# Edge passes of a four-layer graph network: scores and tile maxima of a batch moved into the step before, and a plain running maximum in layer 0

## The chip, the core and the metric

The program runs on one core of one Trainium2 chip. The metric is the device time of one execution in microseconds (us). The engines are PE (matmul; its weight loads are shown as PEld), DVE, ACT, POOL and SP; each runs its own list of instructions in order, and they meet only at semaphores.

## The reference, cut to what matters

A model of four layers works on 3125 nodes of 256 features, with 50000 edges. Each layer adds an edge part, a dense attention part and an expert or MLP part. The change touches only the edge parts that have a softmax over the edges of each node: layer 0 (a directional message, score from the message), layer 1 (dot product of query and key), and the two attention layers of layer 3. In layer 0:

```
messages = (x @ Wf.T)[src] * direction[:, :1] + (x @ Wr.T)[src] * direction[:, 1:2]
scores = leaky_relu(einsum('ef,hf->eh', messages, attn_forward[0]), 0.2)
exp_scores = exp(scores - scores.max(axis=0, keepdims=True))     # one maximum per head, over all edges
sum_exp = segment_sum(exp_scores, dst)
out = segment_sum(messages * exp_scores / (sum_exp[dst] + 1e-10), dst)
```

Layers 1 and 3 instead subtract the maximum over the edges of each node (`segment_max`), exponentiate, and divide by the node's sum.

## The kernel before, in words

The edges have been sorted by node into 416 tiles of 128 edge slots; a tile belongs to one bucket of 128 nodes, and a bucket may begin several tiles. One function, `edge_pass`, runs all four passes: `kind` is "dual" in layer 0 (4 heads), "dot" in layer 1 (8 heads, 32 wide), "add" in L3a (4 heads) and L3b (1 head, 256 wide). A batch is SB = 8 tiles, so there are NB = 52 batches, and a step of the unrolled loop (`steps`) handles one new batch `n` and, LAG = 2 steps later (1 in "dot"), its sums. In each step:

- POOL gathers the rows of 8 tiles by indirect transfer (L1288) into a ring of RING = LAG + 2 slots. A slot is free once the sums of the batch in it are done (`summed`), in "dual" once its message is made (`used`).
- DVE makes the scores (`score_rows`, L1311 to L1339); in "dot" that is a product and a reduction over 2048 columns, in "add" three small instructions, after key matmuls on PE; in "dual" three products and sums over 544 columns.
- PE turns the scores (`turn_scores`, L1488); DVE takes a forward and a backward maximum scan within each tile (`tile_maxima`, L1346, L1347); PE brings the tile maxima to one row (`row_maxima`, L1494 to L1496); DVE scans that row, which carries the open node's maximum from batch to batch (`chain_maxima`, L1354 to L1365); PE brings it back as columns (`column_maxima`, L1503); DVE widens it over the tile (`widen`, L1371 to L1373); PE turns it back (`turn_back`, L1509), DVE subtracts (`lower`, L1380, L1381), ACT exponentiates and weighs (L1622, L1632; on DVE L1391).
- ACT also makes the factor by which old sums fall when the maximum rises (L1614, L1616); PE spreads it (`spread_factor`, L1519, L1520), DVE applies it (`rescale`, L1399).
- For the old batch PE forms 8 tile sums (`sums`, L1533), each into one of BANKS banks, and DVE adds each to the accumulator (`merge`, L1409); a bank is free when its merge is done.
- SP loads the masks of tile borders ("walls", L1273, L1275).

All steps of a batch's maximum, from scores to lowering, lie in one step. The order on DVE is: scores, rescale, merge 0, tile maxima, (weigh), chain, merges 1 and 2, widen, merges 3 and 4, lower, the rest. The order on PE is: as many sums as there are banks, turn, row maxima, one sum, keys, column maxima, two sums, turn back, factor, the rest. In L3b (`guest`) the layer's message MLP runs beside the pass: PE does its whole share of a step between the first three sums and the turn, and BANKS is 3. In "dot" PE also expands query rows (L1482), which ACT copies out (L1607). The order on each engine is written out by hand.

Of the kernel before, what the change touches and what calls it, by code (L numbers as in the profile page):

```python
# [26 lines left out]
ds = bass.ds  # L27
# [15 lines left out]
SB = 8  # L43
# [1101 lines left out]
def edge_pass(kit, name, kind, order, row_table, key_rows, heads, width, acc, guest=None):  # L1145
# [26 lines left out]
    ROW = P  # L1172
    COL = ROW + H * SEQ
    BACK = COL + 2
    KEYS = RING * H
    with Stage(kit, name) as s:
# [4 lines left out]
        hot = s.sb("hot", [P, RING, SB, P])  # L1181
        wall = s.sb("wall", [R, 2, P + 1])
        chain_wall = s.sb("chain_wall", [1, 2, H * SEQ + 1])
        score_all = s.sb("score_all", [P, P])
        score = score_all[:, 0:R]
        shifted = s.sb("shifted", [P, R])
        runs = s.sb("runs", [R, P])
        tops = s.sb("tops", [P, P])
# [4 lines left out]
        ends = s.sb("ends", [1, 2, P])  # L1193
        column = s.sb("column", [R, 2])
        fall = s.sb("fall", [1, H])
        factor = s.sb("factor", [1, H])
        minus = s.sb("minus", [1, 1])
        if kind == "dual":
            dirs = s.sb("dirs", [P, 2, ST])
            msg = s.sb("msg", [P, 2, SB, HALF])  # L1200
            msg2 = s.sb("msg2", [P, SB, HALF])
            rhs = s.sb("rhs", [P, RING, SB, M])
# [25 lines left out]
        def share(units, c):  # L1228

            if beside and 0 <= c < NB:  # L1230
                for _ in range(beside.UNITS * (c + 1) // NB - beside.UNITS * c // NB):
                    next(units)

# [17 lines left out]
        with nc.Block() as block:  # L1251

            @block.sync
            def _(sp):
# [8 lines left out]
                for n in range(NB):  # L1263
                    b = n % 2
                    if keyed:
                        if n >= 2:
                            sp.wait_ge(columns_hot, n - 1)
                        sp.dma_start(lo_rows[:, b, :], order["lo_rows"][n * SB:(n + 1) * SB, :]
                                     .rearrange("t p -> (t p)").partition_broadcast(P)).then_inc(lined[b], 16)
                    if n >= 2:  # L1270
                        sp.wait_ge(widened, n - 1)
# [21 lines left out]
            def _(dve):  # L1293
# [11 lines left out]
                def score_rows(n, c, ring_turn):  # L1305
                    g = rows[:, c % RING]
                    out = by_head(score)
                    dve.wait_ge(gathered[c % RING], ring_turn * (16 * SB) + 16 * SB)
                    if kind == "dot":
# [3 lines left out]
                        if c >= 1:  # L1313
                            dve.wait_ge(lowered, n)
                        v.tensor_reduce(out, g[:, :, 0:KW].rearrange("p k (h v) -> p k h v", h=H), X,
                                        ALU.add).then_inc(scored, 1)
                    if kind == "add":
                        dve.wait_ge(expanded, n * 2 + 2)
                        if c >= 1:
                            dve.wait_ge(factored, n)  # L1320
                        if c >= 1:
                            dve.wait_ge(lowered, n)
# [3 lines left out]
                        v.scalar_tensor_tensor(out=score, in0=score, scalar=0.2, in1=score, op0=ALU.mult,  # L1326
                                               op1=ALU.max).then_inc(scored, 1)
                    if kind == "dual":
                        if c >= 2:
                            dve.wait_ge(weighed_act, n - 1)  # L1330
                        link.note(v.tensor_tensor(msg[:, c % 2], g[:, :, 0:HALF],
                                                  bcast(dirs[:, 0, ds(n * SB, SB)], HALF, 2), ALU.mult))
                        link(v.tensor_tensor(msg2[:], g[:, :, HALF:RW], bcast(dirs[:, 1, ds(n * SB, SB)], HALF, 2), ALU.mult))
                        m = msg[:, c % 2]
                        v.tensor_tensor(m, m, msg2[:], ALU.add).then_inc(used, 1)  # L1335
                        dve.wait_ge(used, n + 1)
                        if c >= 1:
                            dve.wait_ge(lowered, n)
# [3 lines left out]
                def tile_maxima(n, c, wall_turn):  # L1342
                    b = c % 2
                    dve.wait_ge(walled[b], wall_turn * (16 * (H + 1)) + 16 * (H + 1))
                    dve.wait_ge(turned, n + 1)
                    link(v.tensor_tensor_scan(runs[:], wall[:, b, 0:P], ps_a[0:R, 0:P], -BIG, ALU.add, ALU.max))  # L1346
# [2423 lines left out]
```

## Time and profile before

| | us |
|---|---|
| timed runs, median of 3 (lowest, highest) | 8171.8 (8169.69, 8186.81) |
| span of the profiled execution, first to last instruction | 8112.0 |
| profiled execution's own time | not given apart from the span |
| PE, DVE, ACT, POOL busy (share of the span) | 5601.5 (69%), 4057.9 (50%), 2838.0 (35%), 3138.4 (39%) |
| mean granted TensorE clock, share of 2.4 GHz | 0.800 |

Busy time is the time in which an engine executes; the rest it waits or is being given work. The profile is of one execution. Its shares are means over stages with different limits, so the edge passes have to be read from windows of their own. Lines such as L1409 are lines of the kernel; a pass is told from another by the names (L_edges is layer 0 between 1130 and 1900 us and layer 1 between 2838 and 3646 us; L3a_edges and L3b_edges are the others).

### The profile page before, as it was taken

Reading aid. Unit: us, or ns where it says so; the run is one execution under the profiler, and the core shown is the slowest. Engines: PE = TensorE matmul, PEld = TensorE weight load, DVE = VectorE, ACT = ScalarE, POOL = GpSimd, SP = SyncE. Lnnn points to the kernel's source line nnn. Section 1 sums busy time; section 2 is a strip of 40 time slices with the busy share of each in tenths; the row PEclk is TensorE's granted clock in tenths of the full one; section 3 lists DMA queues with packets and bytes.
Section 4 is the critical chain, followed back from the end, with each engine's and each line's share of the span. In section 5 each row is a group of like instructions: output and inputs, shape, how many; then the busy total and the mean of one; then the engine's idle time right before and its main releaser. Section 6 shows DMA issues by size and latency. Waiting matters only on the chain. (4 is left out here: it accounts for less than half of the span.)

```text
span 8112.0 us, 86982 instructions
## 1 busy us (share of the span) xinstructions
PE 5601.5 (69%) x21290; PEld 3555.5 (44%) x21290; DVE 4057.9 (50%) x9795; ACT 2838.0 (35%) x7825; POOL 3138.4 (39%) x3209
## 2 busy tenths in 40 slices
PE   2222547677699778887785568698857866888576
PEld 1111325445355356653343345354545543555343
DVE  5325836665311389994434333423456675555501
ACT  4223627664122144430102333122246633555110
POOL 3663035553466166640005662100056634555011
PEclk9999965557799878778997778799956666787588
DMA  2221521111010255540002221100033423333122
GB/s 84 69 65 42 173 66 43 40 39 16 26 32 20 74 157 159 160 129 14 8 27 87 84 85 39 38 33 30 14 103 106 110 66 92 89 91 90 54 109 69
DMA packets 272398, 573.85 MB, mean 71 GB/s; under 512 B 87398, under 2 KB 138138, under 8 KB 265242
## 3 DMA queue, kind: packets, MB, share of 16 engines
q0 software_dynamic: 134496, 314.63, 15.5%
q1 hardware_dynamic: 137530, 254.96, 9.6%
q8 instruction: 148, 2.42, 0.1%
q14 instruction: 224, 1.84, 0.1%
HBM read 520.14 MB, written 49.19 MB: 70 GB/s over the span
## 5 line engine op out<-in xcount | busy, mean ns | idle before, releaser
L1288 POOL DMA_INDIRECT L_edges_rows<-scratch_L_kv,L_edges_index x416 | 491.1, 1180 | 392.5 <-PE L_edges_ps_sum L1533 221.5
L1288 POOL DMA_INDIRECT L3a_edges_rows<-scratch_L3a,L3a_edges_index x416 | 442.6, 1064 | 472.7 <-DMA L3a_edges_last<-order_dst_last 256.7
L1288 POOL DMA_INDIRECT L3b_edges_rows<-scratch_L3b,L3b_edges_index x416 | 396.8, 954 | 460.1 <-PE L3b_edges_ps_sum L1533 296.7
L1288 POOL DMA_INDIRECT L_edges_rows<-scratch_L,L_edges_index x416 | 416.4, 1001 | 372.2 <-DVE L_edges_msg L1335 199.2
L1730 POOL TENSOR_TENSOR L_norm_fold<-L_norm_square 128x400 f32<-128x400 f32 x64 | 66.5, 1040 | 1262.2 <-ACT L_norm_square L1739 1262.2
L676 POOL DMA_INDIRECT L_edges_rows<-scratch_L,L_edges_index x416 | 396.8, 954 | 394.2 <-SPq L660 145.6
L499 POOL DMA_INDIRECT scratch_by_dst<-dst_record,dst_dest x400 | 406.2, 1016 | 315.0 <-DVE dst_dest L338 195.6
L518 POOL DMA_INDIRECT scratch_by_src<-src_record,src_dest x400 | 387.7, 969 | 266.9 <-issue 110.1
L688 PE MATMUL L_edges_ps_sum<-L_edges_rows,L_edges_hot 128*128 128x256 f32 x832 | 271.1, 466 | 222.7 <-issue 122.8
L400 PE MATMUL rank_ps_count<-rank_parts,rank_ident_b 128*128 128x225 bf16 x200 | 53.6, 370 | 534.6 <-DVE rank_parts L312 423.9
L2376 DVE TENSOR_TENSOR L_experts_gated_h<-L_experts_hidden,L_experts_share_rows 128x800 f32<-128x800 f32 x112 | 111.0, 992 | 609.5 <-ACT L_experts_hidden L2366 535.0
L1409 DVE TENSOR_TENSOR L_acc<-L_edges_ps_sum,L_acc 128x264 f32 (+1 forms) x832 | 357.1, 429 | 97.1 <-DVE L_acc L1409 57.5
L2366 ACT ACTIVATE L_experts_hidden<-L_experts_ps_h,L_eb_sb 128x400 f32<-128x400 f32 x320 | 187.6, 593 | 613.8 <-PE L_experts_ps_h L2328 499.7
L1533 PE MATMUL L_edges_ps_sum<-L_edges_rhs,L_edges_hot 128*128 128x264 f32 x832 | 395.4, 640 | 0.3 <-DVE L_acc L1409 0.3
L1533 PE MATMUL L3a_edges_ps_sum<-L3a_edges_rows,L3a_edges_hot 128*128 128x264 f32 x832 | 373.6, 610 | 1.4 <-DVE L_acc L1409 1.3
L728 DVE TENSOR_TENSOR L_acc<-L_edges_ps_sum,L_acc 128x256 f32 x416 | 176.7, 425 | 380.8 <-DMA scratch_L<-L_table_row 177.4
L464 ACT ACTIVATE rank_apart<-x,rank_key_f 128x128 bf16<-128x128 f32 x800 | 244.4, 388 | 301.2 <-remote 239.1
L2339 PE MATMUL L_experts_ps_o<-L_experts_gated_h,L_e_sb 128*128 128x400 f32 x896 | 330.9, 511 | 23.9 <-DVE L_experts_gated_h L2376 23.9
L1533 PE MATMUL L3b_edges_ps_sum<-L3b_edges_rows,L3b_edges_hot 128*128 128x258 f32 x832 | 333.9, 553 | 5.1 <-DVE L_acc L1409 4.9
L2328 PE MATMUL L_experts_ps_h<-xn,L_e_sb 128*128 128x400 f32 x896 | 323.0, 504 | 2.1 <-PEq L113 2.1
L1596 ACT ACTIVATE L_edges_hot<-iota,L_edges_lo 128x128 f32<-128x128 f32 x832 | 254.7, 386 | 161.9 <-DMA L_edges_last<-order_src_last 92.1
L688 PEld LDWEIGHTS L_edges_ps_sum<-L_edges_rows,L_edges_hot 128*128 128x128 f32 x832 | 173.7, 226 | 313.2 <-issue 178.9
(761 smaller groups left out, 13494.6 us busy)
## 6 DMA issues: line engine op xcount, KB each, us to landing
x<-scratch_dst_key_rows SPq DMA_DIRECT2D x50, 512.0 KB
x<-scratch_src_key_rows SPq DMA_DIRECT2D x50, 512.0 KB
L_experts_w<-in_L_w SPq DMA_DIRECT2D x16, 1024.0 KB
L_edges_rows<-scratch_L,L_edges_index POOLq DMA_INDIRECT x832
L_edges_lo_rows<-order_src_lo_rows SPq DMA_DIRECT2D x52, 256.0 KB
L3a_edges_lo_rows<-order_dst_lo_rows SPq DMA_DIRECT2D x52, 256.0 KB
L3b_edges_lo_rows<-order_dst_lo_rows SPq DMA_DIRECT2D x52, 256.0 KB
x<-scratch_dst_lo_rows SPq DMA_DIRECT2D x50, 256.0 KB
```

Of the source, the lines that this page charges most:

```text
L464: ins = nc.scalar.activation(apart[:, u, k, :], key_line[:, u, k * P:(k + 1) * P], ACT.Abs, scale=-1.0, bias=key_f[:, ds(n * SB + k, 1)])
L499: pool.indirect_dma_start(order["table"], bass.IndirectOffsetOnAxis(order["dest"][:, t:t + 1], 0), order["record"][:, t, :], None).then_in ...
L518: pool.indirect_dma_start(self.order["table"], bass.IndirectOffsetOnAxis(self.order["dest"][:, t:t + 1], 0), self.order["record"][:, t, :] ...
L676: pool.indirect_dma_start(rows[:, n % RING, k, :], None, row_table, bass.IndirectOffsetOnAxis(index[:, t:t + 1].bitcast(U32), 0)).then_inc ...
L688: nc.tensor.matmul(ps_sum[:, k % 4, 0:F], hot[:, n % RING, k, :], rows[:, n % RING, k, :], start=True, stop=True).then_inc(summed, 1)
L1288: pool.indirect_dma_start(rows[:, n % RING, k, 0:RW], None, row_table, bass.IndirectOffsetOnAxis(index[:, t:t + 1].bitcast(U32), 0)).then_ ...
L1409: v.tensor_tensor(a, ps_sum[:, (c * SB + k) % BANKS, 0:M], a, ALU.add).then_inc(merged, 1)
L1533: nc.tensor.matmul(ps_sum[:, (c * SB + k) % BANKS, 0:M], hot[:, c % RING, k, :], values(c)[:, k, :], start=True, stop=True).then_inc(summe ...
L1596: ins = nc.scalar.activation(hot[:, c % RING, k, :], kit.iota[:], ACT.Abs, scale=-1.0, bias=lo[:, ds(n * SB + k, 1)])
L2328: ins = nc.tensor.matmul(ps_h[:, (a + o) % 4, 0:CW], weights[l][:, e, f, o * P:(o + 1) * P], r, start=f == 0, stop=f == len(src) - 1)
L2339: nc.tensor.matmul(ps_o[:, o, 0:CW], weights[hid][:, e, f, o * P:(o + 1) * P], gated_h[:, n % 2, f, :], start=e == 0 and f == 0, stop=False)
L2366: nc.scalar.activation(hidden[l][:, n % 2, o, :], ps_h[:, a % 4, 0:CW], func, bias=biases[l][:, n % EX, o:o + 1]).then_inc(taken, 1)
```

## The change

For every kind, the scores and the tile maxima of batch n+1 are now made in the step that holds the carried chain of batch n (row scan, columns, widening, lowering) and the sums of batch n-LAG. The turned scores move from bank `ps_a` to `ps_c`, where the spread factor and the key products lie, so PE waits for `maxed` before it writes the factor or the next keys. `score` and `tops` get two buffers, `msg` three. `RING` grows by one in L3a only. Key columns, query expansions and their copies run one batch further ahead. `row_maxima` waits for `listed` (the end of `lower`) of the batch before. In L3b the MLP's share of a step is cut into two halves on PE.

In "dual" (layer 0) the maximum is no longer one per node: a running maximum per head over all batches so far replaces it. One reduction takes the place of the two tile scans, one matmul each that of the row and column matmuls, two small instructions that of the chain scans, and the widening, the turn back and the wall loads go.

Core of the diff (long; what is left out renames buffers or changes the prologues in the same sense):

```diff
-    RING = LAG + 2
+    HRING = LAG + 2
+    RING = LAG + 3 if kind == "add" and not guest else HRING
-    AHEAD = 2 if kind == "dot" else 1
+    AHEAD = 3 if kind == "dot" else 2
...
                 def tile_maxima(n, c, wall_turn):
+                    if kind == "dual":
+                        dve.wait_ge(turned, n + 1)
+                        v.tensor_reduce(tops[0:R, b, 0:1], ps_c[0:R, TURN:TURN + P], X, ALU.max).then_inc(maxed, 1)
+                        return
...
                 def chain_maxima(n, c):
                     dve.wait_ge(rowed, n + 1)
+                    if kind == "dual":
+                        old, new = highest[:, 1 - b, :], highest[:, b, :]
+                        link(v.tensor_reduce(new, ps_a[0:1, ROW:ROW + R].rearrange("o (h k) -> o h k", h=H), X, ALU.max))
+                        link(v.tensor_tensor(new, new, old, ALU.max))
+                        if c >= 1:
+                            dve.wait_ge(fell, n)
+                        v.tensor_tensor(fall[:], old, new, ALU.subtract).then_inc(chained, 3)
+                        return
...
# DVE, step
-                    if new:
-                        score_rows(n, c, ring_turn)
                     if old:
                         r = nc.values_load_multi_w_load_instructions(...)
-                        rescale(m, d, r)
-                        merge(m, d, r, (0,))
-                    if new:
-                        tile_maxima(n, c, wall_turn)
-                    if keyed and c + AHEAD < NB:
-                        hot_columns(n + AHEAD, c + AHEAD, wall_turn + (AHEAD + c % 2) // 2)
-                    if LAG == 2 and 1 <= c <= NB:
-                        weigh(n - 1, c - 1)
                     if new:
                         chain_maxima(n, c)
                     if old:
-                        merge(m, d, r, (1, 2))
+                        rescale(m, d, r)
+                        merge(m, d, r, (0,))
+                    if more:
+                        score_rows(n + 1, c + 1, (c + 1) // RING)
+                    if old:
+                        merge(m, d, r, (1,))
                     if new:
                         widen(n, c)
+                    if LAG == 2 and 1 <= c <= NB:
+                        weigh(n - 1, c - 1)
                     if old:
-                        merge(m, d, r, (3, 4))
+                        merge(m, d, r, (2,))
+                    if more:
+                        tile_maxima(n + 1, c + 1, (c + 1) // 2)
+                    if keyed and c + AHEAD < NB:
+                        hot_columns(n + AHEAD, c + AHEAD, (c + AHEAD) // 2)
+                    if old:
+                        merge(m, d, r, (3,))
                     if new:
                         lower(n, c)
                     if LAG == 1 and new:
                         if old:
-                            merge(m, d, r, (5,))
+                            merge(m, d, r, (4, 5))
                         weigh(n, c)
                     if old:
-                        merge(m, d, r, (6, 7) if LAG == 1 and new else (5, 6, 7))
+                        merge(m, d, r, (6, 7) if LAG == 1 and new else (4, 5, 6, 7))
...
# PE: waits
                 def row_maxima(n, c):
                     pe.wait_ge(maxed, n + 1)
+                    if c:
+                        pe.wait_ge(listed, n)
                 def spread_factor(n, c):
+                    if c + 1 < NB:
+                        pe.wait_ge(maxed, n + 2)
# PE, step, after the change
+                    add(0, 1)
+                    column_maxima(n, c)
+                    add(2)
+                    share_part(units, c, True)
+                    expand_pair(n + 2, c + 2, r, 2)      # "dot"
+                    expand_pair(n + 2, c + 2, r, 3)
+                    turn_scores(n + 1, c + 1)
+                    add(3)
+                    turn_back(n, c)                      # not in "dual"
+                    add(4)
+                    spread_factor(n, c)
+                    expand_keys(n + 2, c + 2, r, 0)      # "add"
+                    expand_keys(n + 2, c + 2, r, 1)
+                    row_maxima(n + 1, c + 1)
+                    add(5)
+                    share_part(units, c, False)
+                    add(6, 7)
+                    expand_pair(n + 3, c + 3, r, j)      # "dot", j = 0, 1
...
# ACT, step
-                    if kind == "dot" and c + 1 < NB:
-                        for j in range(4):
-                            copy_asked(n + 1, c + 1, j)
                     if c < NB:
                         fall_factor(n, c)
+                    if kind == "dot" and c + 2 < NB:
+                        for j in range(4):
+                            copy_asked(n + 2, c + 2, j)
+                    if c < NB:
                         weights(n, c)
                         weigh(n, c)
```

## Rows read from the trace of the kernel before

**Rows 1.** Windows of the passes: length, busy PE, PEld, DVE, ACT, POOL, clock, DMA.

```profile
1130.00:1900.00 770.00, 528.69 (x1657) 368.59 (x1657) 488.31 (x1344) 520.78 (x1863) 403.78 (x403) 0.58 0.19 38
...
2838.00:3646.00 808.00, 666.21 (x2463) 482.50 (x2463) 732.65 (x1296) 335.18 (x818) 475.80 (x402) 0.78 0.56 152
...
5930.00:6600.00 670.00, 528.17 (x2053) 377.96 (x2053) 456.22 (x1349) 421.61 (x1446) 420.22 (x393) 0.64 0.40 102
...
6770.00:7550.00 780.00, 669.86 (x2597) 438.60 (x2597) 428.25 (x1367) 420.29 (x1087) 367.97 (x386) 0.78 0.33 83
```

**Rows 2.** Tile sums L1533, one row a pass: ns min/median/max, first and last start.

```profile
L1533 PE MATMUL L_edges_ps_sum<-L_edges_rhs,L_edges_hot x832: 386/647/810, 1174.1 to 1896.9; 128*128 128x264 f32 x167
...
L1533 PE MATMUL L_edges_ps_sum<-L_edges_rows,L_edges_hot x832: 392/393/823, 2858.0 to 3643.9; 128*128 128x272 f32 x167
...
L1533 PE MATMUL L3a_edges_ps_sum<-L3a_edges_rows,L3a_edges_hot x832: 385/647/810, 5954.1 to 6593.0; 128*128 128x264 f32 x167
...
L1533 PE MATMUL L3b_edges_ps_sum<-L3b_edges_rows,L3b_edges_hot x832: 377/636/801, 6792.6 to 7545.7; 128*128 128x258 f32 x167
```

**Rows 3.** Waits of DVE in layer 0: us in total, times, longest.

```profile
DVE L_edges_chain_run L1354 <- DMA x<-scratch_src_key_rows: 51.2, 13, 14.6
```

**Rows 4.** Timeline of layer 0, one pause: start us, length us, idle before.

```profile
1556.00 1.15 ACT L1600 ACTIVATE L_edges_hot<-L_edges_hot,ones 128x1024 f32<-128x1024 f32 x1 [2.19 <-remote]
...
1556.08 0.41 DVE L1346 TENSOR_TENSOR_SCAN L_edges_runs<-L_edges_wall,L_edges_ps_a 32x128 f32<-32x128 f32 x1 [5.96 <-DMA x<-scratch_dst_key_rows]
```

**Rows 5.** Timeline of DVE, a step of layer 0 without pause.

```profile
1505.78 0.71 DVE L1331 TENSOR_TENSOR L_edges_msg<-L_edges_rows,L_edges_dirs 128x544 f32<-128x544 f32 x1
...
1508.76 0.42 DVE L1399 TENSOR_TENSOR L_acc<-L_acc,L_edges_ps_c 128x260 f32 x1 [0.62 <-issue]
...
1510.99 0.28 DVE L1354 TENSOR_TENSOR_SCAN L_edges_chain_run<-L_edges_chain_wall,L_edges_ps_a 1x68 f32<-1x68 f32 x1
...
1511.93 0.41 DVE L1409 TENSOR_TENSOR L_acc<-L_edges_ps_sum,L_acc 128x264 f32 x1
...
1513.10 0.15 DVE L1371 COPY L_edges_column<-L_edges_ps_a 32x2 f32<-32x2 f32 x1
...
1514.20 0.40 DVE L1409 TENSOR_TENSOR L_acc<-L_edges_ps_sum,L_acc 128x264 f32 x1
...
1520.19 0.42 DVE L1399 TENSOR_TENSOR L_acc<-L_acc,L_edges_ps_c 128x260 f32 x1 [0.62 <-issue]
```

**Rows 6.** Timeline of PE in layer 0; two matmul records make one fp32 matmul.

```profile
1503.32 4.77 PE L1533 MATMUL L_edges_ps_sum<-L_edges_rhs,L_edges_hot 128*128 128x264 f32 x10
...
1515.27 0.59 PE L1519 MATMUL L_edges_ps_c<-ones 1*128 1x4 f32 x2
```

**Rows 7.** Timeline of layer 1's start: eighth gather, first use of the batch.

```profile
2827.72 0.95 POOL L1288 DMA_INDIRECT L_edges_rows<-scratch_L_kv,L_edges_index  x1 [0.30 <-issue]
...
2831.55 2.29 DVE L1311 TENSOR_TENSOR L_edges_rows<-L_edges_rows,L_edges_asked 128x2048 f32<-128x2048 f32 x1 [7.46 <-DMA L_edges_rows<-scratch_L_kv,L_edges_index]
```

**Rows 8.** Timeline of layer 1 around lowering.

```profile
3220.43 0.21 DVE L1380 TENSOR_TENSOR L_edges_shifted<-L_edges_score_all,L_edges_ps_a 128x64 f32<-128x64 f32 x1
...
3220.94 1.27 PE L1533 MATMUL L_edges_ps_sum<-L_edges_rows,L_edges_hot 128*128 128x272 f32 x2
...
3221.08 2.28 DVE L1391 TENSOR_TENSOR L_edges_rows<-L_edges_rows 128x2048 f32<-128x2048 f32 x1
...
3222.49 1.70 POOL L1288 DMA_INDIRECT L_edges_rows<-scratch_L_kv,L_edges_index  x1 [1.25 <-PE L_edges_ps_sum L1533]
```

**Rows 9.** Groups of L3a, 6050 to 6500 us: busy us, mean ns, idle.

```profile
L1391 DVE TENSOR_TENSOR L3a_edges_rows<-L3a_edges_rows 128x1024 f32<-128x1024 f32 x35 | 42.2, 1206 | 0.0
...
L1473 PE MATMUL L3a_edges_ps_c<-L3a_sparts,L3a_edges_hot_t 128*128 x280 | 24.5, 175 | 0.5
```

**Rows 10.** Waits of L3b, DVE and PE: us in total, times, longest.

```profile
DVE L3b_edges_runs L1346 <- PE L3b_edges_ps_a L1488: 138.5, 35, 6.3
...
PE L3b_edges_ps_a L1494 <- DVE L3b_edges_tops L1347: 60.2, 44, 4.2
```

More of the change, by code:

```diff
@@ L1232, in share, with share_part, score @@
                     next(units)
+        def share_part(units, c, first):
+            if beside and 0 <= c < NB:
+                count = beside.UNITS * (c + 1) // NB - beside.UNITS * c // NB
+                for _ in range(count // 2 if first else count - count // 2):
+                    next(units)
+        def score(c):
+            return score_all[:, c % 2, :]
         def values(c):
@@ L1306, in score_rows @@
                     g = rows[:, c % RING]
-                    out = by_head(score)
+                    out = by_head(score(c))
                     dve.wait_ge(gathered[c % RING], ring_turn * (16 * SB) + 16 * SB)
@@ L1389, in weigh @@
                     scale = bcast(parts(c)[:, :, act_heads:H, V], V, 3)
-                    src = bcast(msg[:, c % 2, :, 0:V], H - act_heads, 2) if kind == "dual" else out
+                    src = bcast(msg[:, c % 3, :, 0:V], H - act_heads, 2) if kind == "dual" else out
                     v.tensor_tensor(out, src, scale, ALU.mult).then_inc(weighed_dve, 1)
@@ L1454, in _ @@
                 if keyed:
-                    for c in range(AHEAD):
+                    for c in range(2):
                         hot_columns(c, c, 0)
+                score_rows(0, 0, 0)
+                tile_maxima(0, 0, 0)
+                for c in range(2, AHEAD):
+                    if keyed:
+                        hot_columns(c, c, c // 2)
                 steps(step)
@@ L1507, in turn_back @@
                 def turn_back(n, c):
+                    if kind == "dual":
+                        return
                     pe.wait_ge(widened, n + 1)
@@ L1581, in _ @@
                 if kind == "dot":
-                    r = key_registers(1, 0, 4)
+                    r = key_registers(1)
+                    for j in range(4):
+                        expand_pair(1, 1, r, j)
+                turn_scores(0, 0)
+                if kind == "add":
+                    r = key_registers(1)
+                    for j in range(2):
+                        expand_keys(1, 1, r, j)
+                row_maxima(0, 0)
+                if kind == "dot":
+                    r = key_registers(2, 0, 4)
                     for j in (0, 1):
-                        expand_pair(1, 1, r, j)
+                        expand_pair(2, 2, r, j)
                 steps(step)
@@ L1630, in weigh @@
                             out = parts(c)[:, k, h, 0:V]
-                            src = msg[:, c % 2, k, 0:V] if kind == "dual" else out
+                            src = msg[:, c % 3, k, 0:V] if kind == "dual" else out
                             ins = nc.scalar.activation(out, src, ACT.Copy, scale=parts(c)[:, k, h, V:V + 1])
@@ L1635, in step @@
                 def step(n, c, ring_turn, wall_turn):
-                    if kind == "dot" and c + 1 < NB:
-                        for j in range(4):
-                            copy_asked(n + 1, c + 1, j)
                     if c < NB:
                         fall_factor(n, c)
+                    if kind == "dot" and c + 2 < NB:
+                        for j in range(4):
+                            copy_asked(n + 2, c + 2, j)
+                    if c < NB:
                         weights(n, c)
@@ L1649, in _ @@
                 if kind == "dot":
-                    for j in range(4):
-                        copy_asked(0, 0, j)
+                    for c in range(2):
+                        for j in range(4):
+                            copy_asked(c, c, j)
                 steps(step)
```

126 lines of the change are left out of this document (64 added, 62 removed).

## The prediction

> **What bounds the kernel now.** I read the windows of the four edge passes first [rows 1]: they are 3028 us of a span of 8112.0 us, and nothing outside them is touched. None has an engine that is simply full, apart from layer 1, where DVE is busy 732.65 of 808 us. Layer 0's busiest engine is PE with 528.69 of 770, at a mean granted clock of 0.58. So three passes are bound by the order of hand-overs between DVE and PE, and the fourth by DVE's work.
>
> Each pass has 52 batches, one a step, and its tile sums give the step: (1896.9 - 1174.1) / 52 = 13.9 us in layer 0, 15.1 in layer 1, 12.3 in L3a, 14.5 in L3b [rows 2].
>
> In layer 0 most of DVE's idle time stands before the chain scan L1354, 51.2 us in 13 pauses [rows 3], and before the tile scan L1346. The named releaser, a transfer of an earlier stage, is none: L1354 waits for PE alone, which had long finished. Pauses of this sort hit two engines together: DVE comes back at 1556.08 and ACT at 1556.00, the latter before an instruction that waits only for ACT itself [rows 4]. Without a pause DVE's rescale returns after 11.4 us (1508.76 to 1520.19 [rows 5]), so some 2.5 us of the 13.9 are pauses. What causes them I can't read.
>
> The Trainium skill (Runtime: NRT & Kernel Launch, "Instruction fetch mechanics") says that straight code is fetched ahead and a block's crossing is mostly hidden. If so, these pauses aren't fetches and could go wholly; the trace shows no dependence either, and I don't decide by it.
>
> **Layer 0 (dual).** DVE in a step loses: the chain scans with their two copies, 1510.99 to 1511.93 = 0.94 us, for three tiny instructions, which I put at 0.65 (one has at most the length of a scan, at least that of a copy: 0.45 to 0.95); one of two tile scans, 0.41 (the one at 1556.08 [rows 4]); and the widening, 1513.10 to 1514.20 = 1.10 [rows 5]. That is 1.8 us. PE loses a transpose and some of the one-row matmuls, SP its wall loads.
>
> It doesn't follow that the step shortens by 1.8: the new order has a chain of its own. I count from the end of sum 7 of a step, at PE's low clock (1.2 GHz), where a sum takes 4.77 / 5 = 0.95 [rows 6]. DVE merges (to 0.65), the load of the buckets' registers, the 0.62 us idle before 1508.76 [rows 5], now stands here, half of it under the merge (to 0.95), the chain ends at 1.6, rescale and merge 0 at 2.55, the scores of the next batch (1505.78 to 0.62 before 1508.76, so 2.36 [rows 5]) at 4.9. PE has done three sums and the chain's matmul by 3.4 and waits for the transpose until 4.9. Sums 3 and 4 end at 7.25; the factor's four small matmuls (two of them 0.59 [rows 6], all about 0.95) end at 8.2; the row maxima wait for `listed` (7.2) and end at 8.5; sums 5, 6, 7 end at 11.3. At full clock (2.4 GHz) sums cost half, and the step falls to 10.1, where ACT (520.78 / 52 = 10.0 [rows 1]) and POOL (eight times 0.95 + 0.30 [rows 7]) stand. At a clock near 0.65, a little over the 0.58 of before as PE is fuller, I take 11.0 without pauses. So the gain in a smooth step is 0.4 us, not 1.8.
>
> Of the 2.5 us of pauses I keep 1.2: DVE now idles about 2 us in the part where it follows sums 5 to 7 and can be late there, and has fewer instructions. Bounds: all stay (2.5) or none (0). Step 12.2, gain 1.7 x 52 = **-90 us** (-20 to -155).
>
> **Layer 1 (dot).** DVE's work stays as it is, and DVE has next to no waits to lose. But two things get later. (1) Before, sum 5 ran ahead of lowering. Now it stands on PE behind `row_maxima(n+1)`, which waits for `listed(n)`. DVE does merge 4 and then must wait in merge 5, with the weighing of 2.28 us [rows 8] queued behind it, then merges 6, 7 and the next chain. Lowering starts at 3220.43; row maxima could end 0.9 later, a sum takes 0.7 to 1.27 [rows 8], so merge 5 starts at +1.7 to +2.3 instead of +0.95: 1.0 us a step. (2) The ring stays 3 deep while the scores come a step earlier, and sums 5 to 7, which release the last three gathers, come later. With sum 5 at about +1.8, three gathers 1.25 apart end at +5.4, and data lands 2.9 us after an issue ends at the most (2828.67 to 2831.55, the eighth of the first batch [rows 7]): +8.3. DVE wants them at +7.9 (merges and weighing to +5.4, load, chain 1.35, rescale, merge 0). I take 0.3 us (0 to 1.6: a gather of 1.70, as the one at 3222.49 [rows 8], on top). Step 15.1 to 16.4: 1.25 x 52 = **+65 us** (+20 to +150).
>
> **L3a (add).** Chain, tile scans and widening stay, so DVE saves nothing; the ring grows to 5, so gathers keep their lead. The chain as above, with the widening (1.10), a weighing of 1.21 [rows 9] and both tile scans ahead of the factor on PE: `tile_maxima(n+1)` ends at 7.6, factor 8.6, the eight key matmuls at about 0.1 apiece (at most 0.18 [rows 9]) 9.4, row maxima 9.75, sum 7 12.6 at the low clock; at full clock 10.7. At 0.64 [rows 1] this is 12.0 to 12.1, against 12.3: gain 0.4 x 52 = **-20 us** (+30 to -80).
>
> **L3b (add, with the message MLP beside it).** DVE sits idle 138.5 us before the tile scan, since the transpose stands behind the whole share of the MLP on PE, and PE then idles 60.2 us until the scans are through [rows 10]. Halving the share puts PE's work under those scans. PE is busy 669.86 / 52 = 12.9 a step; I count 0.65 of waiting for the chain and 0.35 for the tile maxima of the next batch: 13.9. The ring stays at 4: the last gather, released by sum 7 at 0, issued by 1.85, lands by 4.0 to 4.7, the scores end by 5.4, and PE is busy with the half share until 5.5. That just fits. From 14.5 or 14.6: gain 0.7 x 52 = **-38 us** (+30 to -80).
>
> Prologues do the first scores outside the loop, the same work; three `msg` and two `score` buffers cost nothing. The added wait for `maxed` before the factor is in the chains above.
>
> **Sum.** -90 + 65 - 20 - 38 = -83 us. The profiled span is 8112.0; the median of the timed runs, 8171.8, lies 59.8 above it, and I leave that. 8112.0 + 59.8 - 83 = **8089 us**.
>
> **Rivals.**
> - *The pauses of layer 0 stay whole.* For it: they recur about every second step with the same pattern; against it: L1 has none, with as many DVE instructions. Layer 0 gains 20 instead of 90: 8159.
> - *The waits go wholly, and the clock rises.* PE would be busy 87% of a step of 11.3 in layer 0; layer 1 and L3b, at 82 and 86%, have 0.78 [rows 1]. Then layer 0 takes 10.6 (-172), L3a 11.2 (-57), L3b 13.3 (-62), layer 1 +1.0 (+52): 8172 - 239 = 7933. The Trainium skill (TensorE: Matmul & The Clock Gate, "What's actually happening") has the clock follow PE's recent activity; the trace agrees in that the two fuller passes have the higher clock.
> - *Slower: the late gathers decide.* Where the ring isn't deepened (layer 1, L3b), gathers released by sums 5 to 7 feed scores taken a step earlier. If data lands at lowering + 9.9 (a 1.70 us issue and 2.9 of landing), the wait is 1.9, not 0.3, with merge 5 on top: layer 1 +2.9 x 52 = +150; L3b +30 instead of -38. With layer 0 at -40 and L3a at 0: 8312; with layer 0 at -90: about 8240. It turns the sign from about 0.5 us of waiting in layer 1 if layer 0's pauses stay, and from 1.9 if they go as forecast. For it: POOL in layer 1 takes 475.80 us for 402 gathers, 1.18 each [rows 1]. Against it: on DVE these waits start only after nearly 8 us.
> - That the change doesn't take effect can't be: the order is written out.
>
> **Chances.** Forecast 0.46 (8030 to 8145), pauses stay 0.20, all goes 0.14, late gathers 0.20. Times within 0.2% (16 us), about what can be told from no change, are "same". Faster: 0.45 of the first, 0.10 of the second, 0.14 of the third = 0.69; same 0.01 + 0.08 = 0.09; slower 0.20 + 0.02 = 0.22. The range reaches down to the case in which all goes, and up into the milder part of the slower one: 7930 to 8220.
>
> **What would show it.** Layer 0's sums spaced 12.2 us a batch, with pauses before the chain or the scores; in layer 1 idle time on DVE before merge L1409 with PE as its releaser, some 50 us, and a step over 16; L3b's DVE idle before the tile scan mostly gone, its step under 14.2; L3a within 0.6 of before. I am wrong in the main if layer 1 keeps 15.1 (then 8024), or if layer 0 is below 11 or above 13.4.

## The result: slower by 4.3%, and the profile after

The changed kernel takes 8544.6 us (median of 4 runs, 8526.0 to 8556.2) beside 8178.2 for the kernel before on the same chip: ratio 1.0435 [1.0413, 1.0457]. 8089 was forecast, so the sign was wrong too. The profiled span is 8524.2 us against 8112.0: 412 us more.

The tile sums of the changed kernel (ns min/median/max, first and last start), to be held against [rows 2]:

```profile
L1588 PE MATMUL L_edges_ps_sum<-L_edges_rhs,L_edges_hot x832: 386/644/810, 1167.6 to 1905.2; 128*128 128x264 f32 x167
...
L1588 PE MATMUL L_edges_ps_sum<-L_edges_rows,L_edges_hot x832: 392/497/823, 2879.1 to 4084.5; 128*128 128x272 f32 x167
...
L1588 PE MATMUL L3a_edges_ps_sum<-L3a_edges_rows,L3a_edges_hot x832: 386/644/809, 6404.4 to 7017.2; 128*128 128x264 f32 x167
...
L1588 PE MATMUL L3b_edges_ps_sum<-L3b_edges_rows,L3b_edges_hot x832: 378/383/801, 7220.7 to 7957.1; 128*128 128x258 f32 x167
```

Last start less first start, against [rows 2]: layer 0 +15, layer 1 +420, L3a -26, L3b -17, together +392; the other 21 lie around the passes (13 of them between layer 0's last sum and layer 1's first). By step (a fifty-second): 14.2, 23.2, 11.8, 14.2 us. So the question is layer 1, whose window now reads (columns as in [rows 1]):

```profile
2860.00:4100.00 1240.00, 694.60 (x2452) 497.79 (x2451) 746.96 (x1298) 332.34 (x813) 505.76 (x402) 0.72 0.36 99
```

DVE's busy time barely moved (732.65 in [rows 1]); its waits came. Waits of DVE in that window (us in total, times, longest):

```profile
DVE L_edges_hot_t L1317 <- DMA L_edges_lo_rows<-order_src_lo_rows: 244.9, 49, 6.0
DVE L_acc L1440 <- PE L_edges_ps_sum L1588: 93.7, 57, 2.3
DVE L_edges_rows L1326 <- DMA L_edges_rows<-scratch_L_kv,L_edges_index: 69.5, 50, 3.3
DVE L_edges_runs L1359 <- PE L_edges_ps_c L1529: 40.3, 49, 1.2
```

These four sum to 448 us. The largest stands at an instruction that my prediction never mentions: `hot_columns`, L1317. Timeline of one step, SP's queue and DVE together (start us, length us, idle before):

```profile
3415.37 0.48 DVE L1396 TENSOR_TENSOR_SCAN L_edges_tops<-L_edges_wall,L_edges_column,L_edges_runs 64x128 f32<-64x128 f32 x1
...
3415.88 2.63 SPq L1288 DMA_DIRECT2D L_edges_wall<-order_src_walls  x8
...
3418.55 0.25 SPq L1290 DMA_DIRECT2D L_edges_chain_wall<-order_src_chains  x1
3418.85 0.35 SPq L1281 DMA_DIRECT2D L_edges_lo_rows<-order_src_lo_rows  x1
3422.61 0.75 DVE L1317 TENSOR_SCALAR L_edges_hot_t<-L_edges_lo_rows,node 128x1024 f32<-128x1024 bf16 x1 [4.63 <-DMA L_edges_lo_rows<-order_src_lo_rows]
...
3423.63 0.21 DVE L1409 TENSOR_TENSOR L_edges_shifted<-L_edges_score_all,L_edges_ps_a 128x64 f32<-128x64 f32 x1
...
3426.18 0.44 DVE L1440 TENSOR_TENSOR L_acc<-L_edges_ps_sum,L_acc 128x272 f32 x1 [1.82 <-PE L_edges_ps_sum L1588]
```

SP's loop loads, for each batch, `lo_rows` and then, once the widening of two batches earlier is done, the walls. So `lo_rows` of batch n+3 stands behind `widened` of batch n: it is issued 3.0 us after the widening ends (eight wall issues, one chain issue) and lands by 3.8 us after that. Before, the load went out at the same place of a step, but its user stood in the next step:

```profile
3207.46 0.34 SPq L1268 DMA_DIRECT2D L_edges_lo_rows<-order_src_lo_rows  x1
```

```profile
3215.43 0.72 DVE L1302 TENSOR_SCALAR L_edges_hot_t<-L_edges_lo_rows,node 128x1024 f32<-128x1024 bf16 x1
```

That is 8.0 us of lead (the two rows are from the trace of the kernel before). `AHEAD` 3 in place of 2 moved the user up by a step, and nothing moved the load. In L3a and L3b `AHEAD` is 2 now, the load one step ahead, and no such wait appears.

### The profile page after: what moved, and what is told of

Its sections match the earlier page's. It is cut to its first block and busy times, and to the rows that moved or that the text cites. A ratio compares the mean times of both kernels' runs of the same rounds, so it can differ in the third digit from the quotient of the medians.

```text
span 8524.2 us, 85875 instructions
## 1 busy us (share of the span) xinstructions
PE 5456.9 (64%) x20926; PEld 3363.0 (39%) x20926; DVE 3937.3 (46%) x9479; ACT 2844.9 (33%) x7825; POOL 3170.4 (37%) x3209
## 5 line engine op out<-in xcount | busy, mean ns | idle before, releaser
L1303 POOL DMA_INDIRECT L_edges_rows<-scratch_L_kv,L_edges_index x416 | 523.7, 1259 | 786.7 <-PE L_edges_ps_sum L1588 610.6
L1523 PE MATMUL L_edges_ps_key<-L_q,L_edges_hot_t 128*128 x832 | 314.9, 545 | 228.9 <-ACT L_edges_asked L1673 214.9
L1588 PE MATMUL L_edges_ps_sum<-L_edges_rhs,L_edges_hot 128*128 128x264 f32 x832 | 367.3, 601 | 0.7 <-DVE L_acc L1440 0.7
L1523 PEld LDWEIGHTS L_edges_ps_key<-L_q,L_edges_hot_t 128*128 128x128 f32 x832 | 230.8, 285 | 303.2 <-issue 250.9
L1588 PE MATMUL L3a_edges_ps_sum<-L3a_edges_rows,L3a_edges_hot 128*128 128x264 f32 x832 | 347.8, 563 | 2.3 <-DVE L_acc L1440 1.8
L1698 ACT ACTIVATE L_edges_rhs<-L_edges_msg,L_edges_rhs 128x64 f32<-128x64 f32 x1248 | 320.9, 335 | 83.2 <-issue 67.9
L1588 PE MATMUL L_edges_ps_sum<-L_edges_rows,L_edges_hot 128*128 128x272 f32 x832 | 331.7, 529 | 5.7 <-DVE L_edges_rows L1420 3.4
```

The costliest lines, as they stand in the source:

```text
L1303: pool.indirect_dma_start(rows[:, n % RING, k, 0:RW], None, row_table, bass.IndirectOffsetOnAxis(index[:, t:t + 1].bitcast(U32), 0)).then_ ...
L1523: ins = nc.tensor.matmul(ps_key[:, j % 2, (k % 2) * D:(k % 2 + 1) * D], hot_t[:, c % 2, k * P:(k + 1) * P], key_rows[:, ds(r[k], 1), :].sq ...
L1588: nc.tensor.matmul(ps_sum[:, (c * SB + k) % BANKS, 0:M], hot[:, c % HRING, k, :], values(c)[:, k, :], start=True, stop=True).then_inc(summ ...
L1698: ins = nc.scalar.activation(out, src, ACT.Copy, scale=parts(c)[:, k, h, V:V + 1])
```

## Experiments

Chips differ: the kernel before took 8178, 8097 and 8174 us in three groups of runs and 7290, 7295 and 7292 in three others, each group on one chip. Ratios are always against it on the same chip. The first sort has the pauses of layer 0 that the prediction speaks of, the second has none, and steps of layer 0 are compared only within a sort. Layer 1's step differs little between chips: 15.1 before on both sorts, 23.2 and 23.1 after.

**1. The load alone.** In "dot", SP issues `lo_rows` one batch sooner, ahead of the wait for `widened`.

```
-                    if keyed:  # lo_rows of batch n
+                    ahead = 1 if kind == "dot" else 0
+                    for m in range(n + ahead if n else 0, min(n + ahead + 1, NB)):
...                       # the same wait and load, with m in place of n
```

> The changed kernel with one thing altered: in layer 1 SP issues the 256 KB load of lo_rows for batch n+1 ahead of its wait for the widening of batch n-2, so that it lands a step before hot_columns wants it. Own theory: the 245 us that DVE spends before hot_columns in layer 1 (49 waits of about 5.0 us) are the load's place in SP's queue, 3.0 us behind the end of the widening; they go, and nothing takes their place, so layer 1's step falls from 23.2 to about 18.4 us and the whole from 8545 to about 8300 us. Rival 1, the late gathers decide (they are released by sums 5 to 7 after the lowering): the wait for the load only covered a wait for gathers, the step stays above 22 and DVE's wait at the product L1326 grows from 1.4 to about 5 us. Rival 2, the transfer is slow by itself (landing takes 3.5 us or more beside the gathers): also gone here, since it has a whole step, so only the size would differ.

Measured: 8232 us, 1.0167 [1.0137, 1.0196] of before (8097). Waits of DVE in layer 1, and its sums:

```profile
DVE L_edges_rows L1328 <- DMA L_edges_rows<-scratch_L_kv,L_edges_index: 67.8, 49, 2.7
DVE L_acc L1442 <- PE L_edges_ps_sum L1590: 55.6, 54, 2.3
DVE L_edges_runs L1361 <- PE L_edges_ps_c L1531: 40.3, 49, 1.2
```

```profile
L1590 PE MATMUL L_edges_ps_sum<-L_edges_rows,L_edges_hot x832: 392/393/822, 2855.1 to 3782.1; 128*128 128x272 f32 x167
```

The wait at `hot_columns` is gone, the wait for gathers stayed at 68, the step is 17.8 us: 278 of the 420 us came back, 245 of the wait itself and 38 of merge 5's. Run 7's first variant, which has the same early load, repeats it without pauses: layer 1's step is 23.1 in the changed kernel there and 17.9 with the load early. The load's place in the queue is shown to be the main cause. "The late gathers decide" falls as an account of the 23.2, but 2.7 us a step remain.

**2. Sum 5 first.** As 1, and `add(5)` ahead of `row_maxima` in "dot".

> As the one before, and in layer 1 PE does sum 5 ahead of row_maxima of the next batch, as the kernel before had it ahead of lowering. Own theory: merge 5 no longer waits 1.8 us behind row_maxima's wait for `listed`; the gather it releases is issued earlier. Layer 1's step 18.4 to 16.6 us, the whole some 90 us below the run with the load alone, about 8210 us. Rival: the gathers' landing decides, DVE arrives earlier at the scores and waits there instead (1.4 to 3.2 us), so the step stays at 18.4 and the whole at 8300 us.

Measured: 8253 us, 1.0194 [1.0164, 1.0225]; layer 1's step 18.5, slower than 1. My own theory failed and the rival was too mild: merge 5's wait fell to 16 us, and the wait for gathers doubled.

```profile
DVE L_edges_rows L1328 <- DMA L_edges_rows<-scratch_L_kv,L_edges_index: 139.5, 50, 4.2
```

The gathers show why. POOL and, from another view, the weighing on DVE in the same step:

```profile
3322.11 0.94 POOL L1305 DMA_INDIRECT L_edges_rows<-scratch_L_kv,L_edges_index  x1 [0.30 <-PE L_edges_ps_sum L1590]
3323.35 2.30 POOL L1305 DMA_INDIRECT L_edges_rows<-scratch_L_kv,L_edges_index  x1 [0.30 <-issue]
```

```profile
3322.55 2.28 DVE L1422 TENSOR_TENSOR L_edges_rows<-L_edges_rows 128x2048 f32<-128x2048 f32 x1
```

The gather that starts after the weighing has begun ends 0.8 us after the weighing's end, and the one begun before it isn't stretched. Here the stretched one starts 0.8 us into the weighing and takes 2.30 us; in run 1, 1.2 into it and 1.90. The last gather that the scores need ended 6.9 us after lowering began and not 6.5, and DVE, no longer held at merge 5, came to the scores 1.1 us sooner: together about the 1.4 us a step by which the wait grew. The Trainium skill (SBUF — State Buffer, "Who interferes with whom") says that a VectorE instruction with two inputs in SBUF contends with a GpSimd instruction that reads SBUF, and that the port pair they share is locked by one of them at a time. The weighing has two such inputs and the gather reads its index from SBUF; these rows agree, also in that the gather that came first runs undisturbed.

**3. All sums ahead of the turn.** As 1, and in "dot" another order:

```
 # DVE: rescale, merge 0
+merge(m, d, r, (1, 2, 3))
 score_rows(n + 1, ...); widen(n, c)
+merge(m, d, r, (4, 5))
 tile_maxima(n + 1, ...); hot_columns(n + 3, ...)
+merge(m, d, r, (6, 7))
 lower(n, c); weigh(n, c)
 # PE: add(0, 1), column_maxima(n, c)
+add(2, 3, 4, 5, 6, 7); expand_pair(n + 2, ..., 2)
 turn_scores(n + 1, c + 1)
+expand_pair(n + 2, ..., 3)
```

> The changed kernel with the early load of lo_rows, and in layer 1 alone another order: VectorE does merges 0 to 3 ahead of the scores, 4 and 5 after the widening, 6 and 7 ahead of lowering; TensorE does all 8 sums ahead of turn_scores, and the last pair of query expansions behind it. Own theory: with the load out of the way, what holds layer 1 at 17.8 us is a ring through three engines: the scores of n+1 gate turn_scores, this gates sum 3 to 7 of batch n-1 on TensorE, these gate five gathers of batch n+2 on POOL (lowering + 6.5 us to the last one's end), and their landing gates the scores of n+2. With the sums ahead of the turn the gathers start a score's length (4.6 us) earlier, the 1.4 us wait before the product goes, and with all merges ahead of lowering so does that of 1.07 at merge 5: a step of 14.6 to 15.2 us, bounded by VectorE's work, layer 1 some 140 to 165 us below the early load alone, the whole 8070 to 8095 us where that gave 8232. Rival: the gathers' landing is bound by POOL's work and the stretched gathers themselves (12.1 us a batch), so the wait at the product stays above 1 us and the step above 16.5.

Measured: 7409 us, 1.0163 [1.0147, 1.0180] of 7290. The wait for gathers shrank to a single one:

```profile
DVE L_acc L1442 <- PE L_edges_ps_sum L1590: 80.8, 119, 1.4
DVE L_acc L1442 <- DVE L_acc L1442: 41.9, 193, 0.6
...
DVE L_edges_rows L1328 <- DMA L_edges_rows<-scratch_L_kv,L_edges_index: 0.8, 1, 0.8
```

The loop through three engines (scores of n+1, turn, sums 3 to 7, five gathers, scores of n+2) was real: opened, it takes the wait with it, though the ring is as deep as before. That DVE now waits elsewhere doesn't merely hide it: the batch's last gather ends 1.1 us after lowering began, seven microseconds ahead of its use. (The plain test of the same loop, a ring of four batches for layer 1 too, gave no result: it doesn't fit into SBUF beside the rest.) But the step is 16.75, not 15: DVE now waits at merge 0 behind two pairs of query expansions, and in each row of merges 0.21 us between neighbours.

**4. One pair behind the sums**, merges 4 to 7 interleaved.

> As the run with all sums ahead of the turn in layer 1, whose step was 16.75 us with no wait for gathers left; there VectorE waited 1.19 us at merge 0, since two pairs of query expansions (1.9 to 3.8 us) stood ahead of sum 0 on TensorE, and 0.21 between merges that follow each other directly (four places). Here one of these pairs stands behind the eight sums, and merges 4 to 7 have other work between them. Own theory: 1.0 + 0.6 us a step go, 15.2 us, 80 us in all, layer 1 as fast as before the change (15.1). Rival: the pair moved behind the sums delays the turn and then the tile maxima, since its copy on ScalarE waits for the product; the step stays above 16.

Measured: 8151 us, 0.9974 [0.9959, 0.9990] of 8174; layer 1's step 15.84. Between the two theories: 0.9 of the 1.6 us came (on a chip of the other sort than run 3's). DVE's waits in layer 1:

```profile
DVE L_acc L1442 <- PE L_edges_ps_sum L1592: 86.9, 127, 1.3
DVE L_acc L1442 <- DVE L_acc L1442: 8.4, 37, 0.6
```

The interleaving did its part, 41.9 us between merges in run 3 and 8.4 here. Moving the pair did not: the waits for sums, 80.8 us in run 3, are 86.9, only that they now stand before merges 1 to 3. Layer 1 is still 0.7 us a step slower than the order of before, in which DVE waits for a sum 2.0 us in the whole pass.

**5. All but layer 1.** The new edge pass for layer 0, L3a and L3b, the old one for layer 1.

> The changed edge pass for layer 0, L3a and L3b, the edge pass of before for layer 1. If layer 1 is all of the loss: on a chip with pauses 8178 + 15 - 26 - 17 = 8150, 0.3% below before; on one without, -31 for layer 0 and +7 and +20 for L3a and L3b, the same within 0.1%. Rival: the passes affect what lies around them (prologues, the stages between) and a loss above 0.5% stays.

Measured: 8106.5 us, 0.9910 [0.9894, 0.9926] of 8174, on a chip with pauses; layer 1's step 15.1. So layer 1 is all of the loss. The gain is larger than expected since a trace of before on this chip (span 8161.8) has 14.4 and 12.55 for layer 0 and L3a, against 14.2 and 11.7 in this version.

**6. The changed kernel on both sorts of chip.**

> The changed kernel, unaltered, on the same chip as the trace of before. Where there are no pauses: layer 0 gains only what its smooth step gains, 11.2 to 10.6, 31 us; layer 1 loses 23.2 - 15.1 = 8.1 us a step, 420 us; L3a and L3b (11.72 and 13.79 before without pauses) lose some 5 to 25 us: +400 us on 7290, ratio 1.055. Where there are pauses: as first measured, 1.043 to 1.047.

> The changed kernel unaltered. On a chip without pauses 1.053 to 1.057 of before, the same 420 us of layer 1 and 20 of L3b on a base of 7290, less 30 of layer 0; on one with pauses 1.043 to 1.047. If layer 1's loss belonged to pauses too, it would be smaller without them.

Measured: 1.0448 [1.0427, 1.0469] of 8174, and 1.0626 [1.0610, 1.0642] of 7292, the latter beyond what I expected (against the trace of before with paced gathers, run 7, by passes: -31, +414, +7, +21; 20 more between layer 0's last sum and layer 1's first). Layer 1's loss is the same on both. Layer 0's sums, first the chip with pauses, then the one without:

```profile
L1588 PE MATMUL L_edges_ps_sum<-L_edges_rhs,L_edges_hot x832: 386/644/809, 1171.8 to 1909.1; 128*128 128x264 f32 x167
```

```profile
L1588 PE MATMUL L_edges_ps_sum<-L_edges_rhs,L_edges_hot x832: 386/644/809, 814.2 to 1365.6; 128*128 128x264 f32 x167
```

14.2 against 10.6 us a step in one and the same program: whether there are pauses is decided by the chip or its state, not by the program. A second trace of the kernel before says the same; expected was

> The kernel before, unaltered, for a trace on the same chip as the three others of this group. Layer 0 had pauses on one chip and none on another (13.9 against 11.2 us a step, the whole 8112 against 7291 us). If the pauses belong to the chip, this trace has either all of them (layer 0 near 13.9, the span near 8100) or none (11.2, near 7290), and the changed kernel in the same group the like; if they come by chance from run to run, the two traces and the timed runs differ among themselves by hundreds of us.

and measured 14.4 us a step of layer 0 on the chip where the timed runs are 8174.

**7. What makes layer 0's pauses.** The changed kernel, first the timeline of DVE in one, then of ACT:

```profile
1516.07 0.43 DVE L1440 TENSOR_TENSOR L_acc<-L_edges_ps_sum,L_acc 128x264 f32 x1 [2.23 <-PE L_edges_ps_sum L1588]
1523.19 0.43 DVE L1440 TENSOR_TENSOR L_acc<-L_edges_ps_sum,L_acc 128x264 f32 x1 [6.69 <-DMA scratch_dst_lo_rows<-rank_lo_row]
```

```profile
1518.07 0.35 ACT L1698 ACTIVATE L_edges_rhs<-L_edges_msg,L_edges_rhs 128x64 f32<-128x64 f32 x1 [0.36 <-issue]
1519.47 1.07 ACT L1698 ACTIVATE L_edges_rhs<-L_edges_msg,L_edges_rhs 128x64 f32<-128x64 f32 x3 [1.04 <-issue]
1520.90 0.35 ACT L1698 ACTIVATE L_edges_rhs<-L_edges_msg,L_edges_rhs 128x64 f32<-128x64 f32 x1 [0.36 <-issue]
```

DVE stops for 6.7 us, in every second step; ACT, which waits for nobody here, gets one to three instructions at a time. First, ScalarE with 16 weighing instructions a batch in place of 24 (`act_heads` 2):

> The changed kernel, with ScalarE weighing two of layer 0's four heads instead of three (16 instructions a batch instead of 24), VectorE two instead of one in the same single instruction. It asks about layer 0's pauses of 6.5 us in every second step (29.0 us for two steps, each pause 82 traced DVE instructions after the last). Theory A, ScalarE's stream of instructions is what starves: a third fewer of its weighing instructions, pauses shorter or rarer, layer 0's step from 14.2 to 12.5 to 13. Theory B, VectorE's own stream sets the pause: its count of instructions is unchanged, the pause stays at every 82nd, two steps stay at 29 us, and the whole at 8545 us or a few us more, as the one DVE instruction grows by 0.3 us. Theory C, ScalarE's load in layer 0 (532.8 us busy) bounds the smooth step: it falls from 11.0 to about 10.5.

Measured on a chip with pauses: 1.0451 [1.0419, 1.0484]; layer 0's step 13.0 in place of 14.0 (run 1, same chip), but the smooth steps grew to 11.2 to 12.0, so the pauses fell from 3.0 to about 1.4 us a step. B is out, and so is C. Then POOL's gathers spread over the step, by `pool.wait_ge(summed, (n - RING - 3) * SB + k + 1)` in "dual", and the like in the kernel before:

> The changed kernel with the early load of lo_rows (whose layer 0 step is 14.0 us: 11.0 and 17.7 in turn), and in layer 0 alone each gather waits as well for the tile sum of seven batches earlier, so that POOL issues its 8 gathers of a batch spread over a step and not 16 in one run of 21 us. They still lead the scores by three batches. Theory P, the pauses of VectorE and ScalarE come from POOL's long run of gathers (in the pause at 1516 us both engines come back when the run of 16 ends): the pauses go or fall below 1 us a step, layer 0's step comes to 11.2 to 11.8 us, the whole to 8090 to 8120 us on a chip where the early load alone gave 8232. Theory A, what starves is each engine's own stream of instructions (two of three heads on ScalarE shortened the pauses, 14.2 to 13.0): POOL's spacing doesn't matter, the step stays at 13.9 to 14.2 and the whole at 8232.

> The kernel before, with the same pacing in layer 0 (each gather waits for the tile sum of six batches earlier), nothing else. Theory P: its pauses (13.9 us a step against 11.4 in a smooth one) go as well: layer 0's step 11.6, the whole 2.3 x 52 = 120 us below the kernel before. Theory A: no difference, within 0.3%.

Both ran on a chip without pauses, so neither tests P against A as meant. There the pacing changes nothing: 0.9999 [0.9990, 1.0009] for before; 1.0238 [1.0221, 1.0255] for the changed kernel with the early load, whose layer 0 takes 10.6 us a step paced as unpaced (runs 7 and 3). The unpaced changed kernel on a chip without pauses (run 6) does say something: POOL gathers there without a break from 1049 to 1110 us, and DVE never waits longer than 2.8 us. A long run of gathers alone makes no pause. The two paced runs also gave what layer 0 takes without pauses: 11.2 us a step before, 10.6 after. Two heads and one head on ScalarE, in the version of 5:

> The changed edge pass for layer 0, L3a and L3b, that of before for layer 1, and ScalarE weighs two of layer 0's heads, VectorE two. On a chip with pauses layer 0's step goes from 14.2 to 13.0 as it did alone, -60 us, so the whole comes to 0.991 - 0.007 = 0.984 of before. On a chip without pauses the smooth step decides: ScalarE gets 8 instructions shorter and VectorE's one grows by 0.54 us, 10.6 becomes 10.6 to 11.2, the whole the same as without it or up to 30 us slower, 0.999 to 1.003.

> As the one before, with one head on ScalarE (8 weighing instructions a batch) and three on VectorE. Theory A, the number of ScalarE's instructions sets the pauses: they go on shortening with the second 8 instructions taken away, layer 0's step on a chip with pauses is 11.8 to 12.5 us. Theory S, what helped was that ScalarE got slack (532.8 to 419.2 us busy) and with one head it has more slack but VectorE's single instruction grows to 1.76 us on the chain from scores to lowering: a smooth step of 11.7 or more, the pauses as with two heads, a step of 13.4 or more. On a chip without pauses both give 11.2 to 11.9.

Measured, again without pauses: two heads 1.0042 [1.0028, 1.0055], a step of 10.9, a little over my range; one head 1.0080 [1.0066, 1.0093] and, on a second such chip, 1.0074 [1.0059, 1.0089], a step of 11.3 and 11.2. So fewer instructions on ScalarE cost time where there are no pauses. A against S is open, since no run of one head met a chip with pauses.

**8. The best version.** Layer 0 and L3a changed, layer 1 and L3b as before:

> The changed edge pass for layer 0 and L3a alone; layer 1 and L3b, whose step was 13.8 us before and 14.2 after where there are no pauses, as before. On a chip with pauses -13 (layer 0) and -39 (L3a): 0.993 to 0.995 of before, 13 us above the version with L3b changed too. On one without: layer 0 11.2 to 10.6, L3a unchanged: 0.996 of before, where the versions with L3b changed lost.

Measured without pauses: 7276.7 us, 0.9978 [0.9968, 0.9987] of 7292, faster than both kernels, by half of what was expected. In the same group the version of 5 gave 1.0023 [1.0013, 1.0033], inside the 0.999 to 1.003 expected of it: L3b, 13.8 a step before, is 14.3 in it. With pauses, 5 is the fastest that was run; this one wasn't run there.

## Why the prediction was wrong, point by point

**What failed: "Layer 1 ... Step 15.1 to 16.4".** The part lists two things that get later and misses a third, the key columns of batch n+3, moved up a step past a queue that wasn't moved. I had the diff's `AHEAD` before me and counted nothing for it. Run 1 prices it: 5.4 us a step, 278 us, of the 366 by which the medians differ. Without it the kernel is still slower, by 1.7%.

**The terms that I did count in layer 1 were undersized.** Merge 5 behind `row_maxima`: 1.0 foreseen, 1.82 in the timeline while the load was late too, 1.07 in run 1 (55.6 / 52). The gathers: 0.3 us foreseen, 1.3 measured (67.8 / 52). I charged the gathers behind sums 5 to 7 alone, but sums 3 and 4 too stand behind `turn_scores(n+1)`, so five gathers are late and the last is issued in full 6.5 us after lowering. A third, 0.8 us (40.3 / 52) for the turn behind the query pairs, I didn't have. Without the late load the step is 17.8, 2.7 above before; my slower rival said 2.9 a step, +150 us, and its bill was nearly right (+141), in part by luck: it had 1.9 for the gathers, where 1.3 were measured, and nothing for the turn. The other 5.4 us are in none of my rivals.

**Layer 0, -90 foreseen, +15 measured.** The smooth step was right: 11.0 counted, 11.0 in the trace (between the pauses), 10.6 in the mean of a pass without them. "Of the 2.5 us of pauses I keep 1.2" failed: they are 3.2 (14.2 - 11.0). That idle time would absorb them was only argued. The rival in which they stay whole was the better one, and even that was 0.7 short. But that the change makes them grow isn't shown: on the chip of runs 5 and 6 the kernel before has 14.4 and the changed one 14.2. What all traces of the new layer 0 with pauses share is a longer first step, 38 us or more from one rescale to the next, where before it is 16.4. On a chip without pauses the part is worth 11.2 - 10.6 = 0.6 a step, 30 us, not 90.

**L3a, -20 foreseen, -26 measured.** Right on the first chip, but by luck: without pauses before and after are 11.7 and 11.85, so my reason, a shorter chain, gained nothing, and what L3a gains are pauses. The sum was also off in itself: 12.3 less the 12.0 to 12.1 that I counted is 0.2 to 0.3, not 0.4.

**L3b, -38 foreseen, -17 measured.** The wait ahead of the tile scan [rows 10] did go; in its place DVE waits for sums (67.1 us before) and for gathers, and PE for the chain, for which I had counted 0.65 us a step:

```profile
DVE L_acc L1440 <- PE L3b_edges_ps_sum L1588: 238.4, 127, 5.4
DVE L3b_edges_key_sum L1335 <- DMA L3b_edges_rows<-scratch_L3b,L3b_edges_index: 29.1, 27, 1.7
...
PE L3b_edges_ps_a L1554 <- DVE L3b_edges_fall L1386: 62.3, 40, 5.3
```

"That just fits" was 0.5 us too kind to the last gather, and the chain costs PE 1.2 us a step here and 1.5 without pauses (78.1 us in run 6), about what the wait ahead of the tile maxima had cost it before [rows 10]. Without pauses the part is a loss of 0.4 us a step.

**"Prologues do the first scores outside the loop, the same work"** was put at nothing. Without pauses there are 20 us more between layer 0's last sum and layer 1's first, and 5 where layer 1 is as before (the version of run 5), so layer 1's new start costs about 15. With pauses this can't be read: 13 and 10 us more in the changed kernel, 10 with layer 1 as before.

**The clock** granted was 0.62, 0.72, 0.70 and 0.80 in the four passes (windows from 1130, 2860, 6390 and 7190 us), against [rows 1] up in three and down in layer 1, where PE's busy share fell from 0.82 to 0.56. The rival in which all waits go and the clock rises didn't come: no pass lost its waits.

## What to carry to other kernels

When a use is moved up by a step, list every input of it and where that is issued: a queue that works in order and waits for an event of this step serves a use of this step late, whatever the buffers. When a producer of a batch is moved up but the ring isn't deepened, follow the loop once round (scores, turn, sums, gathers, scores) and add it up; the longest such loop bounds the step. And where DVE is busy nine tenths of a step, as in layer 1, an overlap of its own work with itself has nothing to give, and new waits are paid nearly in full (3.1 us of them a step in run 1, 2.7 us of step).

## What the runs showed of the hardware

The same program took about 7290 us in three groups of runs and 8097 to 8178 in three others. Of the 870 us between two traces of the order of before, some 360 lie ahead of layer 0, 170 in layer 0, and 150 in layer 2's edge pass, which the change doesn't touch (12.9 against 10.1 us a step); in the latter two passes the traces with pauses put most of DVE's stops down to transfers of an earlier stage, as in [rows 3]. In the ordering stage ahead of layer 0 a trace of the kernel before with pauses has this wait of DVE, which isn't among the large ones of the trace without (the paced kernel of before):

```profile
DVE x L318 <- remote: 343.4, 23, 27.6
```

Layer 0's first sum starts at 1170.5 us in the one and 811.3 in the other. What the pauses are isn't settled: DVE and ACT stop together, fewer instructions on ScalarE shortened them, and a long run of gathers alone doesn't make them. No run here excludes the fetching of instructions. A gain found on one sort can be a loss on the other (L3b: 14.5 to 14.2 with pauses, 13.8 to 14.2 without).

The stretching of a gather by a VectorE instruction already under way (0.95 to 2.30 us in the rows of run 2) turned an earlier release into a later landing. It isn't the weighing's alone. In run 3 a gather that starts 0.2 us into the product of the scores takes 2.92 us and again ends 0.8 us after it, and the next one, issued during the reduction, which has one input, takes its usual 0.94:

```profile
2707.16 2.28 DVE L1328 TENSOR_TENSOR L_edges_rows<-L_edges_rows,L_edges_asked 128x2048 f32<-128x2048 f32 x1
2709.47 2.29 DVE L1330 TENSOR_REDUCE L_edges_score_all<-L_edges_rows 128x64 f32<-128x2048 f32 x1
```

```profile
2707.34 2.92 POOL L1305 DMA_INDIRECT L_edges_rows<-scratch_L_kv,L_edges_index  x1 [0.30 <-issue]
2710.55 0.94 POOL L1305 DMA_INDIRECT L_edges_rows<-scratch_L_kv,L_edges_index  x1 [0.30 <-issue]
```
